# A rank-one term of the attention scores moved from 64-row tiles to 32-row tiles of TensorE

## The reference

```
k, v = split((x @ w_kv_down) @ w_kv_up)          # 16 heads of 64
q    = x @ w_q
att  = einsum('bqhd,bkhd->bhqk', q, k) * 64**-0.5
att  = where(causal, att, -inf)
y    = einsum('bhqk,bkhd->bqhd', softmax(att), v) @ w_out
```

## Time and profile before

| | us |
|---|---|
| median of three runs | 2446.82 |
| lowest, highest | 2445.96, 2450.33 |
| the profiled execution | 2450.61 |
| its span, first to last instruction | 2449.0 |
| TensorE busy | 2204.8 (90% of the span) |
| VectorE, ScalarE, GpSimd busy | 1342.6, 1094.9, 1433.2 |
| mean granted TensorE clock | 0.957 of full speed |

### The profile page before, as it was taken

The page is one execution under the profiler, slowest core; times in us unless marked ns, Lnnn a source line. Parts: engine busy times, 40 slices in busy tenths (PEclk is TensorE's granted clock), DMA queues, the critical chain, the costliest instruction groups (busy, mean ns, idle before and its releaser), DMA issues.

```text
span 2449.0 us, 37319 instructions
## 1 busy us (share of the span) xinstructions
PE 2204.8 (90%) x14896; PEld 1420.5 (58%) x14896; DVE 1342.6 (55%) x1902; ACT 1094.9 (45%) x2159; POOL 1433.2 (59%) x818
## 2 busy tenths in 40 slices
PE   5787558989999999999989999989999999999677
PEld 3565345656666656566555666656666656565355
DVE  4566346565656564656475556475656565654222
ACT  3665423434444444444434444444444444444454
POOL 0233204656777767677656676757676766768412
PEclk9899869989999999999999999989999999999889
DMA  3000000000000000000000000000000000000001
GB/s 99 1 1 0 2 14 7 1 7 1 7 1 8 1 8 1 7 1 7 1 7 1 8 1 8 1 7 1 7 1 8 1 7 1 1 1 1 13 25 44
DMA packets 12218, 19.82 MB, mean 8 GB/s; under 512 B 1168, under 2 KB 9488, under 8 KB 12048
## 3 DMA queue, kind: packets, MB, share of 16 engines
q1 hardware_dynamic: 12048, 17.44, 2.3%
HBM read 13.24 MB, written 4.19 MB: 7 GB/s over the span
## 4 chain that ended last, share of the span: by engine, by line
PE 76%; DVE 14%; ACT 5%; POOL 3%; issue 2%; DMA 0%; POOLq 0%; ACTq 0%; DVEq 0%
PE heads_out L759 18%; PE beside L568 16%; PE two_heads L709 8%; PE scores L743 5%; PE scores L736 5%; DVE part_max L955 5%; PE scores L745 5%; PE scores L747 5%; PE scores L568 4%; PE beside L768 2%; PE two_heads L568 2%; PE two_heads L713 2%; DVE rden L969 2%; PE scores L740 2%; PE beside L722 1%
## 5 line engine op out<-in xcount | busy, mean ns | idle before, releaser
L1199 POOL TENSOR_TENSOR acc<-acc,prob 128x1024 f32<-128x1024 f32 (+3 forms) x512 | 1015.2, 1983 | 203.1 <-ACT prob L1114 148.2
L955 DVE TENSOR_REDUCE part_max<-two_heads 128x2 f32<-128x1024 f32 (+3 forms) x640 | 678.4, 1060 | 550.6 <-PE two_heads L709 277.9
L1114 ACT ACTIVATE prob<-scores 128x512 f32<-128x512 f32 (+3 forms) x1280 | 584.3, 538 | 626.3 <-PE scores L747 503.0
L759 PE MATMUL heads_out<-prob,V 128*64 128x512 f32 (+3 forms) x2560 | 549.1, 550 | 0.0
L709 PE MATMUL two_heads<-k_hi,q_hi 64*128 64x512 f32 (+3 forms) x1280 | 279.0, 430 | 38.7 <-DVE part_max L955 34.3
L759 PEld LDWEIGHTS heads_out<-prob,V 128*64 128x64 f32 x2560 | 157.3, 138 | 225.3 <-issue 201.6
L1194 POOL TENSOR_TENSOR acc<-prob 128x768 f32<-128x768 f32 (+1 forms) x64 | 144.0, 2250 | 197.8 <-ACT prob L1114 197.7
L709 PEld LDWEIGHTS two_heads<-k_hi,q_hi 64*128 64x128 f32 x1280 | 122.4, 186 | 224.6 <-issue 142.9
L743 PE MATMUL scores<-q_hi,k_lo 64*128 64x512 f32 (+3 forms) x1280 | 248.8, 382 | 0.0
L969 DVE RECIPROCAL rden<-rden 128x128 f32<-128x128 f32 x256 | 240.4, 941 | 10.9 <-ACT rden L1125 10.9
L736 PE MATMUL scores<-q_hi,k_hi 64*128 64x512 f32 (+3 forms) x1280 | 245.5, 378 | 0.8 <-ACT neg_max L1103 0.8
(11 more groups left out here) (301 smaller groups left out, 3174.2 us busy)
## 6 DMA issues: line engine op xcount, KB each, us to landing
wP_raw<-wPair SPq DMA_DIRECT2D x16, 384.0 KB, 3.0
X<-u SPq DMA_DIRECT2D x8, 512.0 KB, 9.0
out<-X SPq DMA_DIRECT2D x8, 512.0 KB, 2.9
wA_sb<-wA SPq DMA_DIRECT2D x1, 768.0 KB, 7.6
wFa<-wF SPq DMA_DIRECT2D x1, 768.0 KB, 7.8
wFb<-wF SPq DMA_DIRECT2D x1, 768.0 KB, 4.2
gamma_beta<-gb SPq DMA_DIRECT2D x1, 256.0 KB, 4.6
prob<-wKD SPq DMA_DIRECT2D x1, 128.0 KB, 2.1
```

Source lines behind the costliest of these rows:

```text
L759: made = pe.matmul(heads_out[head(h), x0:], V[(idx - j + c) % NVS][:, tt, head(h)], prob[step % NPROB][:, h, x0:], start=t == 0, stop=t == ...
L955: ve.reduce_max(part_max[:, t, :, c:c + 1], two_heads[:, :, 0:width], AX.X).then_inc(empty(task)[0], 1)
L1114: ac.activation(prob[step % NPROB][:, h, x0:], bank(task, h)[:, x0:], ACT.Exp).then_inc(empty(task, h)[0], 1)
L1199: po.tensor_tensor(total[:, :, x0:], total[:, :, x0:], new[:, :, x0:], ALU.add).then_inc(acc_ok, 1)
```

## The change

L747 leaves the task `score`. A new task `minus` follows the two `score` tasks of a round and adds the minus maximum of both steps and both heads in four matmuls of 32 rows each, at rows 0, 64, 32 and 96: TensorE is in tiles of 32 rows x 128 columns for them. For this the maximum must stand in rows 32 and 96 of `neg_max` as well, so L964 becomes two small reductions, and `sel` has ones in four rows. The wait for `turn_max`, which stood ahead of a unit's first scores, stands ahead of `minus`. All four banks of a round are now released to ScalarE by these four matmuls.

```diff
@@ Plan.attention
             for step in steps[s:s + 2]:
                 self.need("score", *step)
+            if s < len(steps):
+                self.need("minus", *steps[s])
             if at < goal:
                 maximum()
@@ tensor_program, score
-                    w.wait_ge(*empty(("turn_max", idx)))
...
-                    for h in range(2):
-                        pe.matmul(bank(task, h)[:, x0:], sel[head(h), :], neg_max[i][head(h), x0:], start=False, stop=True).then_inc(full(task, h)[0], 1)
+                elif kind == "minus":
+                    idx = task[1]
+                    w.wait_ge(*empty(("turn_max", idx)))
+                    for e in range(2):
+                        step = ("score", idx, task[2] + e)
+                        x0 = P * max(0, task[2] + e - TPB * UNITS[idx][2])
+                        for h in range(2):
+                            rows = slice(h * DH + e * QUAD, h * DH + (e + 1) * QUAD)
+                            pe.matmul(bank(step, h)[:, x0:], sel[rows, :], neg_max[idx % NQ][rows, x0:], start=False, stop=True,
+                                      tile_position=(h * DH + e * QUAD, 0)).then_inc(full(step, h)[0], 1)
@@ vector_program, minus_max
-                    ve.reduce_max(row_max[:, :, :, 0:1], part_max[:, :, :, 0:j + 1], AX.X).then_inc(row_max_ok, 1)
+                    for e in range(2):
+                        made = ve.reduce_max(row_max[:, :, :, e * QUAD:e * QUAD + 1], part_max[:, :, :, 0:j + 1], AX.X)
+                    made.then_inc(row_max_ok, 1)
@@ gpsimd_program, attention_start
-                    for h in range(2):
-                        po.memset(sel[h * DH:h * DH + 1, :].bitcast(F32), 1.0).then_inc(att_const, 1)
+                    for i in range(4):
+                        po.memset(sel[i * QUAD:i * QUAD + 1, :].bitcast(F32), 1.0).then_inc(att_const, 1)
```

More of the change, by code:

```diff
@@ L21 @@
 NH, DH = 16, 64
+QUAD = 32
 NPAIR = NH // 2
@@ L906, in vector_program @@
                     w.wait_ge(ffn["a"]["x_plus_ffn"], 2 * NBL)
-                    w.wait_ge(att_const, 4)
+                    w.wait_ge(att_const, 6)
                     for a in range(2):
```

## The result

The changed kernel takes 2512.93 us (median of four runs, 2509.41 to 2519.22), the kernel before 2446.39 us beside it: a ratio of 1.0272, with a 95% interval of 1.0247 to 1.0297. It is 2.7% slower. The forecast was 2509 us.

What follows compares the result with a forecast made beforehand. TensorE was taken to bound the attention; +67 us there, less 12 hidden, plus 7 lost at `beside` made +62 us, and 2446.8 + 62 = 2509 us, with 8 in 10 for 2455 to 2560 us.

Steps and rivals of the forecast that it cites:

- 67 - 12 = 55 us: On TensorE: 195.6 us added against 128.6 removed gives +67 us, less 12 us hidden in waits for VectorE.
- TensorE bounds the attention: In the attention PE is busy 95% of 1970 us, so nearly everything TensorE saves or loses counts in the end.
- L747 removed, 128.6 us: On TensorE: the removed L747 pairs, priced by width at 0.23, 0.17, 0.12 and 0.11 us, free 128.6 us.
- Four side by side: In minus on TensorE: four 32-row matmuls stream as one, 66.6 us in all, a gain of at most 62.0 us.
- rival C: In minus on TensorE: the four matmuls go only two by two, adding 67 us, 2576 us; chance 6%.
- A change costs 0.21 us: On TensorE: each of 630 added tile-shape changes costs 0.10 us ahead and 0.11 us behind, also between 64 and 32 rows.
- rivals A: On TensorE: a change between 64 and 32 rows is free, so the kernel gains 50 us, 2397 us; chance 14%.
- B: On TensorE: a change costs half, load pulled ahead or drain avoided but not both, 2449 us, no difference; chance 3%.
- 0.11 at the maximum behind it: On TensorE: the maximum that follows a minus group takes 0.11 us longer because the tile shape changes.
- 12 us hidden behind VectorE: At the maximum: a later TensorE waits less for VectorE's reduction, taking 12 us off, between nothing and 26 us.
- the row that was to show it: In the profile after: the maximum's waits for VectorE should shrink by about 12 us in total.
- 7 us lost at `beside`: At `beside`: exponentials 0.92 us later delay the second task in 46 rounds, costing 7 us, between 0 and 41.

Runs made afterwards that it cites:

- short reductions: VectorE's reduction for the maximum reads only half of each head's columns: kernel before 2381.52 us, changed kernel 2471.48 us, minus behind the second maximum 2445.54 us.
- Experiment 3: Changed kernel with all four minus matmuls at rows 0 and 64, so the second step's pair must follow the first's: 2560.35 us, ratio 1.0472.
- Experiment 1: Changed kernel with minus still at the end of the round but in 64-row tiles, adding no change of shape: 2451.32 us, ratio 1.0028.
- experiment 4: Changed kernel with minus moved behind the round's second maximum: first kernel, 32-row tiles, 2535.69 us; second, 64-row tiles, 2520.93 us.
- experiment 6: Changed kernel with minus at the round's end in 64-row tiles and half reductions for the maximum: 2402.18 us, ratio 0.9821.
- experiment 2: Kernel before with the L747 of every round's second step in 32-row tiles at rows 0 and 64, nothing moved: 2549.07 us, ratio 1.0426.

## Why the prediction was right

The time came within 4 us and for the main reason given: the added changes of shape cost more than the side-by-side saves. That it came so close is in part luck. For TensorE's groups themselves the forecast had 67 - 12 = 55 us and the distances give 31 + 24 - 9 = 46; for the late release it had 7, and waits and the rest took 16. Two misses of 9 us cancel.

- **TensorE bounds the attention: right.** Every kernel here moved with TensorE's distances: what lies outside the stretch of the table is 507 to 513 us in all of its columns.
- **L747 removed, 128.6 us:** its distances sum to 145, of which 11 are waits for the reduction behind it; 134 remain with short reductions. The forecast's 128.6 was 5 us too low for the groups themselves, and took the narrowest from neighbours that no maximum follows (0.11 us, where L747 stood at 0.28).
- **Four side by side: right.** Groups of 512 columns took 0.43 us as forecast, and `minus` sums to 135 us, where the forecast had 0.43 x 256 + 0.32 x 64 = 131. Experiment 3 took the side-by-side away and lost 62 us of streaming; rival C falls.
- **A change costs 0.21 us, also between 64 and 32 rows: right in kind.** The loads weren't pulled ahead, so rivals A and B fall. Ahead of `minus` 31 us were measured for a forecast 32. Behind it 24 for 33: the step "0.11 at the maximum behind it" was read at a maximum followed by scores. By the medians it is 0.10 where a projection follows (157 times), 0.06 at 512 columns with the mask behind (60) and 0.11 at 256 columns with the mask (60). In running kernels a change cost 0.165 to 0.177 us.
- **12 us hidden behind VectorE: the size about right, the row that was to show it wrong.** 9 us are hidden in the distances of `minus`. But the waits in the table of names did not shrink (34.3 and 64.0 us before, 35.2 and 66.6 after), as I had said they would. Nor is it that those names take in maxima elsewhere in a round: directly behind `minus` they are 22.4 and 34.4 us before, 22.3 and 35.7 after. Gaps like the one at 1205.60 are mostly too short for that view, so the 9 us are read from the distances alone.
- **7 us lost at `beside`: right where nothing else is short, too narrow in its reason.** Experiment 1 gives 6.6 us. I had counted rounds whose first task is a query or a key. The row of experiment 4 shows a wait behind `turn_max`, which I had left out, and waits over 0.56 us grew by 14 us in the changed kernel. What the late release costs is no constant: 7 us at full reductions, 21 with short ones, 11 in experiment 3; the forecast's account of it is right in kind and not shown in size.
- **The other side would have needed a price under 0.10 us a change.** It is above 0.16 in both kernels that only add changes.

What stays open: with minus behind the second maximum, 34 us of waits over 0.56 us more than its base remain with short reductions. Late exponentials may cause some, as they do at full reductions (the row with 1.32 us); how many, and how many are the reduction still, no run separates.

## What to carry to other kernels

Before TensorE work is packed into smaller tiles, count the changes of tile shape that it adds and price them by two neighbouring groups in the kernel's own timeline: here 0.10 us ahead, up to 0.11 us of exposed weight load behind, 0.17 to 0.18 us in the end. Running two groups of 0.23 us as one saves 0.23 us, which pays for one added change and not for two, and a task in a shape of its own between two neighbours of another shape adds two. And a group moved "to where it costs nothing" also takes itself away from where it gave another engine time: look at what stood on both sides of it for the bank they share. A distance longer than that of the same shape elsewhere can be a wait too short for the view of waits; it is time that the change may take for nothing.

## What the runs showed of the hardware

Four 32-row matmuls, into four banks, start within 0.01 us of each other and stream in the time of one (0.43 us between two changes, the same as a group of two). The four starts lie that close in all 320 groups of the changed kernel.

TensorE's clock fell after one of its own waits. In experiment 4's first kernel the wait of 1.32 us ends at 1267.17; from 1268.6 on the granted clock is 0.50, the 1.2 GHz level, and a pair of 512 columns takes 0.43 us in place of 0.23:

```profile
1269.69 0.63 PE L745 MATMUL scores<-q_hi,k_lo 64*128 64x512 f32 x2
1270.12 0.63 PE L747 MATMUL scores<-q_lo,k_hi 64*128 64x512 f32 x2
```

Busy us of PE, PEld, DVE, ACT and POOL, then the granted clock:

```profile
1262.00:1266.00 4.00, 3.85 (x32) 2.23 (x28) 3.76 (x4) 1.84 (x4) 0.00 (x0) 1.00 0.00 0
1266.00:1268.60 2.60, 1.43 (x12) 1.42 (x12) 0.26 (x1) 1.61 (x4) 1.84 (x1) 1.00 0.03 6
1268.60:1271.80 3.20, 3.20 (x16) 2.47 (x16) 2.08 (x2) 0.60 (x1) 0.53 (x1) 0.50 0.00 0
```

If the wait brought the lower level about, it cost more than its own length; no run changes the one without the other, so that is not shown.

How much time the lower level can have taken is worked out from the table's last row. A pair takes 0.43 us there for 0.23, so at most about half of the time at 1.2 GHz is lost. By this estimate the clock holds up to 9 us of the change's 62 (99 against 82 us at the lower level), up to 24 of the 64 that the short reductions gained, where I had seen 40 (34 against 82), up to 15 of the 90 of the change with short reductions (65 against 34), up to 10 of the 21 of the late release in experiment 6 (55 against 34), up to 9 of the 11 between experiments 2 and 3 (106 against 89) and up to 10 of the 15 between the two kernels of experiment 4 (113 against 92). So the smaller differences of this document, those of the late release above all, may be clock for a good part; the 104 us of experiment 2, with 7 us more at the lower level than before, are not.
